# Segment attention on one NeuronCore: the value product moved ahead of the scores

## The chip, the cores and the metric

The kernel runs on one core of one Trainium2 chip. The metric is the device time of one execution in microseconds (us). Three executions of the kernel before took 755.57, 755.27 and 754.94 us; the median is 755.27 us.

## The reference

Two transformer layers act on 32 batches of 32 tokens of width 256 (1,024 tokens). The change concerns one block of the second layer, `_L1_attn_ref`: two self-attentions over the same tokens, one over all keys of a batch ("lt", long) and one over the keys of the token's own segment ("st", short), then a fusion.

```python
def _mha(x, w_in, b_in, w_out, b_out, n_heads, mask=None):
    qkv = x @ w_in.T + b_in
    q, k, v = jnp.split(qkv, 3, axis=-1)          # 16 heads of 16
    scores = jnp.einsum('bhqd,bhkd->bhqk', q, k) / jnp.sqrt(dh)
    if mask is not None:
        scores = jnp.where(mask[:, None, :, :], scores, -1e9)
    attn = jax.nn.softmax(scores, axis=-1)
    out = jnp.einsum('bhqk,bhkd->bhqd', attn, v)
    return out @ w_out.T + b_out
long_out = _mha(x, lt_w_in, ...)
seg = jnp.argmax(x @ protos.T, axis=-1)           # 8 segments
same = seg[:, :, None] == seg[:, None, :]
short_out = _mha(x, st_w_in, ..., mask=same)
short_out = jnp.where((tok_cnt == 1)[..., None], x, short_out)
combined = jnp.concatenate([long_out, short_out], axis=-1)
return combined @ fus_w.T + fus_b
```

Before it stand the first layer and a cross attention, behind it a layer of eight experts with two chosen for each token.

## The kernel before

The 1,024 tokens are 8 tiles of 128 tokens (4 batches each). Segment attention works in 16 units: unit n is tile n // 2, "lt" where n is even and "st" where it is odd. Each engine runs its own program of steps u, written out by hand in `pe_step`, `act_step`, `dve_step` and `pool_step`; engines meet only at semaphores, and each engine takes its own instructions in the order written. A step works on several units at once. Step u projects queries and keys of unit u+2, makes scores and the value product of unit u+1, and weighs the values of unit u. Even steps (s == 0) also make the segment logits of the next tile; odd steps (s == 1) transpose the one-hot segments of the next tile ("hot") and multiply them into the mask ("same").

One unit goes through the engines like this. TensorE: `project_qk` (helper line L837). ScalarE: kT (L2053) and qT (L2058) out of PSUM. GpSimd: the block-diagonal keys kbd (`spread_heads`, L853, two instructions). TensorE: the scores (`per_batch`, L877, 32 small matmuls) into `s_banks`. VectorE: `off_maximum` (L2219, L2220 for even units; L2226, L2230, L2231 for odd ones). ScalarE: the exponential (L2023). VectorE: `turn`, a transpose (L914). Beside this TensorE makes the value product (`project_tokens`, L846) into `v_part`, ScalarE copies it out (`act_v`, L2008) and GpSimd spreads it (`spread_batches`, L860). TensorE weighs the values (`values`, L904), ScalarE copies the result (`act_own`, L2013, L2016), VectorE normalises and transposes it (`features`, L2188, L2189, L937). `last_y` (L2149, L2154), `act_y` (L2029), `short` (L2242), `fused_near`, `fused_far` (L2161, L2167) and `add` (L2248) finish a tile. `norm_stats` (L2173 to L2176), `root` (L1973) and `norm_apply` (L2182) prepare a tile three ahead.

The value product shares PSUM bank 1 with three other results, the logits (L2107), the transposed one-hot (L2102) and the mask product (L2119). They take turns: each writer waits on the semaphore `vb_done` until the one before it has been read. The turns are counted by `v_use`, in this order:

```python
            if there(t + 1):
                v_use[("logits", "hot")[s], t + 1] = len(v_use) + 1
            if there(u + 1, U):
                v_use["v", u + 1] = len(v_use) + 1
            if s == 1 and there(t + 1):
                v_use["same", t + 1] = len(v_use) + 1
```

So in an even step the value product waits until VectorE has read the logits (`argmax`, L2200 and L2201; L2201 releases them), in an odd step until ScalarE has copied the one-hot (L2045), and the mask product waits until ScalarE has copied the value product (L2008). In `dve_step` the order is `features`, `turn`, `argmax`, `norm_stats` or `norm_apply`, then `off_maximum`.

Seven even steps have logits (u from 0 to 12). They are called logit steps below, the first to the seventh; their L2201 begin at 506.14, 518.23, 532.15, 545.45, 558.62, 571.80 and 586.51 us.

Of the kernel before, what the change touches and what calls it, by code (L numbers as in the profile page):

```python
# [25 lines left out]
NB, SQ, D, SK = 32, 32, 256, 257  # L26
# [40 lines left out]
def at_least(eng, sem, value):  # L67

    if isinstance(value, int) and value <= 0:
        return  # L70
    eng.wait_ge(sem, value)
# [770 lines left out]
def project_tokens(nc, dst, lhs_T, weight):  # L842

    n = weight.shape[1]
    for k in range(n):
        ins = nc.tensor.matmul(dst[:, 0:D], lhs_T[:, k, :], weight[:, k, :], start=(k == 0), stop=(k == n - 1))  # L846
    return ins
# [21 lines left out]
def per_batch(nc, dst, left, right, col, first):  # L869

    for m in range(KT):
        for b in range(BT):
            for f in range(2):
                lo, at = 64 * f, col + P * m
                ins = nc.tensor.matmul(dst[SQ * b:SQ * b + SQ, f, at:at + P], left(lo, m, b), right(lo, m, b),  # L877
                                       start=first and m == 0, stop=True, skip_group_check=True)
    return ins


def tokens(xT):

    return lambda lo, m, b: xT[lo:lo + 64, m, SQ * b:SQ * b + SQ]


def heads_apart(bd):

    return lambda lo, m, b: bd[lo:lo + 64, m, b, :, :].rearrange("p h k -> p (h k)")
# [1013 lines left out]
class SegmentAttention:  # L1903


    def __init__(self, nc, in_wn, in_shared, sem, psum, bank, c, x, w, loaded):
# [4 lines left out]
        def sb(name, shape):  # L1911
            return (in_wn if name in IN_WN or name[0:-1] in IN_WN else in_shared).take(shape)

        column, xT = in_shared.take([P, KT]), in_shared.take([P, NT, KT, P])
        self.turned, self.kept_end = xT, in_shared.at
        U = 2 * NT
        kinds = ("lt", "st")
# [5 lines left out]
        v, vbd = sb("v", [P, D]), [sb(f"vbd{i}", [P, 2 * NG, 2, 33]) for i in range(2)]  # L1923
# [13 lines left out]
        v_part, same_part = v_bank[:, 0:D], v_bank[:, D:D + SQ]  # L1937
# [8 lines left out]
        vb_full, vb_done = sem("vb_full"), sem("vb_done")  # L1946
# [8 lines left out]
        f_use, v_use = {}, {}  # L1955
# [136 lines left out]
        def pe_step(pe, u):  # L2092
# [21 lines left out]
            if there(u + 1, U):  # L2114
                scores(pe, u + 1)
# [14 lines left out]
                fused_far(pe, t - 1)  # L2130

        def scores(pe, n):
            pe.wait_ge(kbd_ready, n + 1)
            pe.wait_ge(q_ready, n + 1)
            at_least(pe, s_read, n)
            per_batch(nc, s_banks, tokens(qT[n % 2]), heads_apart(kbd[n % 2]), 0, True).then_inc(s_full, 1)
            at_least(pe, vb_done, v_use["v", n] - 1)
            project_tokens(nc, v_part, xT[:, n // 2], w[kinds[n % 2] + "_qkv"][:, :, 2 * D:3 * D]) \
                .then_inc(vb_full, 1)

        def values(pe, n):
            pe.wait_ge(pT_ready, n + 1)
# [802 lines left out]
```

## Time and profile before

| | before |
|---|---|
| median of 3 executions | 755.27 us |
| span of the profiled execution, first to last instruction | 751.1 us |
| segment attention's scores, first to last | 500.3 to 597.7 us |
| TensorE busy over the span | 662.8 us (88%) |
| VectorE busy over the span | 485.5 us (65%) |
| ScalarE busy over the span | 365.0 us (49%) |
| GpSimd busy over the span | 310.1 us (41%) |

The span is what the profiler saw of one execution. The profile gives no device time of its own for it; the median of the executions is 4.2 us longer than its span. In the views PE is TensorE's matmuls, PEld its weight loads, DVE VectorE, ACT ScalarE, POOL GpSimd. The value product is two matmuls in the program; the trace shows four, since fp32 matmuls appear in passes.

### The profile page before, as it was taken

Reading aid. Unit: us, or ns where it says so; the run is one execution under the profiler, and the core shown is the slowest. Engines: PE = TensorE matmul, PEld = TensorE weight load, DVE = VectorE, ACT = ScalarE, POOL = GpSimd, SP = SyncE. Lnnn points to the kernel's source line nnn. Section 1 sums busy time; section 2 is a strip of 40 time slices with the busy share of each in tenths; the row PEclk is TensorE's granted clock in tenths of the full one; section 3 lists DMA queues with packets and bytes.
Section 4 is the critical chain, followed back from the end, with each engine's and each line's share of the span. In section 5 each row is a group of like instructions: output and inputs, shape, how many; then the busy total and the mean of one; then the engine's idle time right before and its main releaser. Section 6 shows DMA issues by size and latency. Waiting matters only on the chain.

```text
span 751.1 us, 16917 instructions
## 1 busy us (share of the span) xinstructions
PE 662.8 (88%) x6115; PEld 500.4 (67%) x6115; DVE 485.5 (65%) x1367; ACT 365.0 (49%) x992; POOL 310.1 (41%) x458
## 2 busy tenths in 40 slices
PE   4899999999999989985994799988999776999990
PEld 3677878787777778753443586667877673777760
DVE  2686777677768669885488873558888875333330
ACT  1454545545555479874395653436566431222320
POOL 1235455646453179850000031136556513556541
PEclk9999999999999999996997699999999986999995
DMA  8723222322220000019200434538001022243434
GB/s 265 245 62 79 64 78 65 78 65 75 68 72 14 1 3 4 3 44 332 103 0 1 156 125 177 217 125 367 2 3 65 3 99 53 47 69 58 68 40 70
DMA packets 31697, 65.08 MB, mean 87 GB/s; under 512 B 5792, under 2 KB 21792, under 8 KB 29312
## 3 DMA queue, kind: packets, MB, share of 16 engines
q1 hardware_dynamic: 26016, 55.73, 22.8%
q0 software_dynamic: 4688, 7.18, 6.0%
q10 hardware_dynamic: 912, 1.10, 0.5%
q8 instruction: 50, 0.82, 0.5%
q14 instruction: 31, 0.25, 0.1%
HBM read 57.67 MB, written 7.37 MB: 87 GB/s over the span
## 4 chain that ended last, share of the span: by engine, by line
PE 64%; DVE 21%; ACT 5%; issue 4%; DMA 2%; SPq 2%; POOL 1%; DVEq 0%; ACTq 0%; POOLq 0%
PE psum L2627 7%; PE psum L474 6%; PE psum L482 6%; PE psum L496 5%; PE psum L2637 4%; PE psum L521 4%; PE psum L507 4%; PE psum L1482 3%; PE psum L1459 3%; PE psum L837 2%; DVE ff_peak L1500 2%; PE psum L846 2%; PE psum L829 2%; PE psum L877 2%; DMA wn<-in_w_down 2%
## 5 line engine op out<-in xcount | busy, mean ns | idle before, releaser
L415 ACT ACTIVATE prob<-s_sb,negm 128x257 f32<-128x257 f32 x128 | 66.2, 517 | 94.5 <-DVE negm L640 94.5
L782 POOL TENSOR_SCALAR bias<-dist,cst 128x257 f32<-128x257 f32 x128 | 59.8, 486 | 99.5 <-DVE dist L627 89.6
L636 DVE CUSTOM_DVE_ANT_0 s_sb<-psum,bias 128x257 f32<-128x257 f32 x128 | 49.4, 423 | 51.7 <-PE psum L496 48.4
L474 PE MATMUL psum<-ctxT,shared 128*128 128x257 f32 x256 | 62.6, 388 | 2.7 <-DMA msk<-in_mask 2.7
L482 PE MATMUL psum<-shared,ctxT 128*128 128x256 f32 x256 | 60.4, 379 | 0.0
L2627 PE MATMUL psum<-ex_w,shared 128*128 x184 | 58.3, 460 | 0.6 <-ACT shared L2520 0.6
L1721 POOL TENSOR_TENSOR wn<-wn,cst 128x1 f32<-128x1 f32 x8 | 4.7, 589 | 120.4 <-DVE wn L1848 120.4
L474 PEld LDWEIGHTS psum<-ctxT,shared 128*128 128x128 f32 x256 | 47.2, 195 | 9.0 <-issue 3.4
L482 PEld LDWEIGHTS psum<-shared,ctxT 128*128 128x128 f32 x256 | 48.4, 189 | 6.8
L496 PE MATMUL psum<-kT,qbd 64*128 64x257 f32 x256 | 48.4, 429 | 3.0 <-DVE mx L636 2.9
L2627 PEld LDWEIGHTS psum<-ex_w,shared 128*128 128x128 f32 x184 | 33.1, 190 | 15.4 <-issue 0.8
L2810 DVE TENSOR_TENSOR shared<-psum,shared 128x352 f32<-128x352 f32 x23 | 12.1, 525 | 48.2 <-ACT shared L2536 48.2
L1459 PE MATMUL psum<-shared,ff_used_up 128*128 128x512 f32 x96 | 41.6, 593 | 0.0
L853 POOL TENSOR_TENSOR shared<-shared,cst 128x512 f32<-128x512 f32 x32 | 35.0, 1115 | 7.8 <-ACT shared L2053 6.8
L521 PE MATMUL psum<-pT,v 128*64 128x128 f32 x512 | 35.0, 279 | 2.8 <-DVE o_keys L689 2.8
L2536 ACT ACTIVATE shared<-psum 128x352 f32<-128x352 f32 x23 | 10.7, 464 | 52.8 <-PE psum L2627 52.8
L521 PEld LDWEIGHTS psum<-pT,v 128*64 128x64 f32 x512 | 27.4, 136 | 13.2 <-issue 13.1
L507 PE MATMUL psum<-cst,prob 128*128 128x128 f32 x256 | 35.0, 280 | 0.0
L496 PEld LDWEIGHTS psum<-kT,qbd 64*128 64x128 f32 x256 | 22.3, 184 | 18.6 <-DVE mx L636 10.1
L2637 PE MATMUL psum<-ex_w,shared 128*128 x138 | 33.7, 380 | 0.8 <-DVE shared L2801 0.8
L507 PEld LDWEIGHTS psum<-cst,prob 128*128 128x128 f32 x256 | 27.4, 141 | 10.5 <-issue 10.5
L837 PE MATMUL psum<-shared,late 128*128 128x128 f32 x256 | 33.2, 285 | 0.0
(359 smaller groups left out, 1655.9 us busy)
## 6 DMA issues: line engine op xcount, KB each, us to landing
ctxT<-in_ctx_T SPq DMA_DIRECT2D x32, 257.0 KB
ex_w<-in_w SPq DMA_DIRECT2D x1, 5632.0 KB, 17.5
kpos<-in_kpos SPq DMA_DIRECT2D x32, 128.5 KB
msk<-in_mask SPq DMA_DIRECT2D x32, 128.5 KB
near_turned<-in_ctx_T_tiles SPq DMA_DIRECT2D x4, 1028.0 KB
ff_used_up<-in_ctx_T_tiles SPq DMA_DIRECT2D x4, 1028.0 KB
near_rows<-in_ctx_tiles SPq DMA_DIRECT2D x4, 1024.0 KB, 8.0
ff_used_up<-in_ctx_tiles SPq DMA_DIRECT2D x4, 1024.0 KB, 7.3
```

Source lines behind the costliest of these rows:

```text
L415: nc.scalar.activation(prob[n % 2][:, g, :], s_sb[n % 2][:, g, :], ACT.Exp, bias=negm[:, b, g:g + 1], accum_out=esum[t % 2][:, b, g:g + 1]) \
L474: ins = nc.tensor.matmul(kv[m][:, 0:SK], w["xa_k"][:, k, P * m:P * m + P], ctxT[n % BT][:, k, :], start=(k == 0), stop=(k == KT - 1))
L482: ins = nc.tensor.matmul(kv[0][:, D * i:D * i + D], ctxT[n % BT][:, k, P * i:P * i + P], w["xa_v"][:, k, :], start=(i == 0 and k == 0), st ...
L496: nc.tensor.matmul(sc[g % 2][:, 0:SK], qbd[t % 2][lo:lo + 64, g // 2, b, :, :].rearrange("p h q -> p (h q)"), kT[n % 2][lo:lo + 64, g // 2 ...
L507: ins = nc.tensor.transpose(pt[j][:, at:at + P], prob[n % 2][:, g, P * i:P * i + P], c.ident)
L521: ins = nc.tensor.matmul(oo[64 * half:64 * half + 64, at:at + P], v[n % BT][:, i, 64 * g:64 * g + 64], pT[n % 2][:, g, i, :], start=(n % 2 ...
L636: nc.vector.tensor_tensor_reduce(s_sb[n % 2][:, g, :], sc[g % 2][:, 0:SK], bias[n % 2][:, g, :], 1.0, float("-inf"), ALU.add, ALU.max, mx[ ...
L782: nc.gpsimd.tensor_scalar(bias[n % 2][:, g, :], dist[n % 2][:], c.slope[:, g:g + 1], 1.0, ALU.mult, ALU.mult).then_inc(bias_ready, 1)
L837: ins = nc.tensor.matmul(dst[:, P * m:P * m + P], weight[:, k, P * m:P * m + P], xT[:, k, :], start=(m == 0 and k == 0), stop=True, skip_g ...
L1459: ins = nc.tensor.matmul(bank[2 + n % 6][:], wt[:, k, P * m:P * m + P], xT[:, k, 512 * h:512 * h + 512], start=(k == 0), stop=(k == KT - 1))
L2627: ins = nc.tensor.matmul(y_bank[part][:, 0:FE], rT[j % 2][:, k, :], ex.w1[:, bass.ds(e, 1), k, FE * part:FE * part + FE].rearrange("p a f ...
L2637: ins = nc.tensor.matmul(o_bank[j % 2][:, 0:D], gT[j % 2][0:n, ch, :], ex.w2[0:n, bass.ds(e, 1), ch, :].rearrange("p a d -> p (a d)"), sta ...
```

## The change

In `scores` the value product and its wait are written ahead of the scores and their waits. Nothing else is altered; the counts of `v_use` stay.

```diff
         def scores(pe, n):
+            at_least(pe, vb_done, v_use["v", n] - 1)
+            project_tokens(nc, v_part, xT[:, n // 2], w[kinds[n % 2] + "_qkv"][:, :, 2 * D:3 * D]) \
+                .then_inc(vb_full, 1)
             pe.wait_ge(kbd_ready, n + 1)
             pe.wait_ge(q_ready, n + 1)
             at_least(pe, s_read, n)
             per_batch(nc, s_banks, tokens(qT[n % 2]), heads_apart(kbd[n % 2]), 0, True).then_inc(s_full, 1)
-            at_least(pe, vb_done, v_use["v", n] - 1)
-            project_tokens(nc, v_part, xT[:, n // 2], w[kinds[n % 2] + "_qkv"][:, :, 2 * D:3 * D]) \
-                .then_inc(vb_full, 1)
```

On TensorE a logit step reads as follows, with - for before and + for after; the rows are the logits, queries and keys, scores (L877), value product (L846), the values of the unit before, and the first product of `last_y`.

```order
 L2107 MATMUL psum<-late,shared 128x8 x2
 L837 MATMUL psum<-shared,late 128x128 x8
-L877 MATMUL psum<-shared 32x128 x16
-L846 MATMUL psum<-late,shared 128x256 x2
+L846 MATMUL psum<-late,shared 128x256 x2
+L877 MATMUL psum<-shared 32x128 x16
 L904 MATMUL psum<-shared,wn 64x2x33 x16
 L2149 MATMUL psum<-shared 128x128
```

The value product, with the wait that it carries, has gone ahead of the 32-column scores and stands directly behind the queries and keys. An odd step, with the transposed one-hot (L2102) ahead and the mask product (L2119) behind, reads:

```order
 L2102 MATMUL psum<-cst,shared 8x128
 L837 MATMUL psum<-shared,late 128x128 x8
-L877 MATMUL psum<-shared 32x128 x16
-L846 MATMUL psum<-late,shared 128x256 x2
+L846 MATMUL psum<-late,shared 128x256 x2
+L877 MATMUL psum<-shared 32x128 x16
 L2119 MATMUL psum<-shared 32x32 x4
 L904 MATMUL psum<-shared,wn 64x2x33 x16
```

Here the scores have come between the value product and the mask product. This exchange is made 16 times, once for each unit. The orders of VectorE, ScalarE, GpSimd and the DMA queues are the same as before.

## Rows read from the trace of the kernel before

**Rows 1.** The page: busy us (share of the span) of each engine
```profile
PE 662.8 (88%) x6115; PEld 500.4 (67%) x6115; DVE 485.5 (65%) x1367; ACT 365.0 (49%) x992; POOL 310.1 (41%) x458
```

**Rows 2.** Chain that ended last, 543 to 559 us: start, us, what
```profile
545.45 0.24 DVE shared L2201
...
547.03 0.70 DVE shared L2226
...
548.48 0.79 DVE shared L2231
...
550.66 0.46 DVE shared L2242
...
553.84 0.61 DVE shared L2219
```

**Rows 3.** Timeline of TensorE, fourth logit step and the odd step behind
```profile
542.75 2.03 PE L837 MATMUL psum<-shared,late 128*128 128x128 f32 x16
544.71 0.67 PE L877 MATMUL psum<-shared 64*32 64x128 f32 x32
545.73 1.13 PE L846 MATMUL psum<-late,shared 128*128 128x256 f32 x4 [0.35 <-DVE shared L2201]
546.79 0.70 PE L904 MATMUL psum<-shared,wn 64*64 64x66 f32 x32
...
551.44 1.13 PE L846 MATMUL psum<-late,shared 128*128 128x256 f32 x4
553.03 0.26 PE L2119 MATMUL psum<-shared 8*32 8x32 f32 x8 [0.46 <-ACT shared L2008]
```

**Rows 4.** Timeline, the first scores: TensorE's row and VectorE's
```profile
500.26 0.67 PE L877 MATMUL psum<-shared 64*32 64x128 f32 x32 [0.34 <-POOL shared L853]
...
501.03 0.69 DVE L2219 TENSOR_REDUCE shared<-psum 128x16 f32<-128x512 f32 x1 [1.72 <-PE psum L877]
```

**Rows 5.** Timeline of ScalarE, fourth logit step: exponential, copy of the one-hot
```profile
549.35 0.63 ACT L2023 ACTIVATE wn<-shared 128x512 f32<-128x512 f32 x1 [0.24 <-DVEq L2233]
...
550.77 0.25 ACT L2045 COPY shared<-psum 8x128 f32<-8x128 f32 x1
```

**Rows 6.** Timeline, second logit step: TensorE, VectorE and ScalarE
```profile
518.74 0.88 PE L877 MATMUL psum<-shared 64*32 64x128 f32 x32
...
519.81 0.69 DVE L2226 TENSOR_TENSOR shared<-psum,shared 128x512 f32<-128x512 f32 x1
...
522.95 0.63 ACT L2023 ACTIVATE wn<-shared 128x512 f32<-128x512 f32 x1
```

**Rows 7.** Timeline, sixth logit step: VectorE and GpSimd
```profile
573.08 0.68 DVE L2226 TENSOR_TENSOR shared<-psum,shared 128x512 f32<-128x512 f32 x1
574.10 1.04 POOL L860 TENSOR_TENSOR shared<-shared,cst 128x512 f32<-128x512 f32 x1
574.51 1.17 DVE L2231 TENSOR_TENSOR shared<-shared 128x512 f32<-128x512 f32 x1
```

**Rows 8.** Timeline of VectorE and TensorE, seventh logit step
```profile
586.51 0.23 DVE L2201 TENSOR_SCALAR shared<-psum,shared 128x8 f32<-128x8 f32 x1
588.02 0.68 DVE L2226 TENSOR_TENSOR shared<-psum,shared 128x512 f32<-128x512 f32 x1
...
586.79 1.13 PE L846 MATMUL psum<-late,shared 128*128 128x256 f32 x4 [1.34 <-DVE shared L2201]
```

**Rows 9.** Timeline of GpSimd, fourth logit step: the two spreads of the keys
```profile
547.67 2.48 POOL L853 TENSOR_TENSOR shared<-shared,cst 128x512 f32<-128x512 f32 x2
```

**Rows 10.** The same, in a stretch that ends within the pair
```profile
547.67 1.04 POOL L853 TENSOR_TENSOR shared<-shared,cst 128x512 f32<-128x512 f32 x1
```

**Rows 11.** Waits, 480 to 625 us: total us, times, longest
```profile
PEld psum L2119 <- ACT shared L2008: 6.9, 8, 0.9
```

**Rows 12.** Stretch of 5 us (third from last: mean granted clock); TensorE's longest wait
```profile
600.00:605.00 5.00, 3.74 (x46) 3.62 (x47) 4.49 (x11) 2.32 (x7) 2.25 (x6) 0.66 0.01 3
...
601.26 1.16 PE L904 MATMUL psum<-shared,wn 64*64 64x66 f32 x32 [2.20 <-DVE wn L914]
```

## The prediction

> **What bounds the kernel now.** First the page's busy times: TensorE is busy for 88% of the span and VectorE for 65% [rows 1]. By this alone an exchange on TensorE that keeps its work the same should cost nothing, and TensorE would be the engine to relieve. The chain of waits says otherwise for this stretch. In segment attention the work that ends last runs through VectorE: the release of the logits (L2201), the odd unit's scores off their maximum (L2226 and L2231), through ScalarE to `short` (L2242), and later the even unit's scores (L2219) [rows 2]. Its only break in a pair of steps lies between the end of L2231 at 549.27 and L2242 at 550.66, where ScalarE takes the exponential and then `act_y`. The timeline of TensorE shows the reverse side: in the same pair it waits twice, 0.35 us ahead of the value product, for L2201, and 0.46 us ahead of the mask product, for ScalarE's copy of the value product [rows 3]. So VectorE, with ScalarE's exponential between, sets the pace, and TensorE has about 0.8 us to spare in the 13.2 from one logit step to the next. What counts is when TensorE hands VectorE its scores.
>
> **The change, part by part.** Nothing is added or removed. The value product takes 1.06 us from its start to the start of what follows (545.73 to 546.79) [rows 3], and 16 scores are put behind it. The exchange itself is worth nothing: the same two blocks take their time in either order. I judge each unit by when its scores now arrive and when VectorE wants them.
>
> How late can scores be? VectorE waited for scores once: they began at 500.26 and VectorE's L2219 at 501.03 [rows 4]. From the start of scores to the start of VectorE's work on them is thus 0.77 us.
>
> *Logit steps (seven).* Here the value product waits for L2201. That was so before too, but the scores had already gone: 544.71 in the fourth logit step, when L2201 had not begun [rows 2, 3]. Now they queue behind the waiting product. L2201 begins at 545.45 and the product 0.28 us later; 1.06 us later come the scores, and 0.77 us later L2226. That is 0.28 + 1.06 + 0.77 = 2.11 us from the start of L2201 to the start of L2226, where it was 547.03 - 545.45 = 1.58 us [rows 2]. The work of VectorE between them (three small operations and the statistics of `norm_stats`) covers only the 1.58. So L2226 comes 0.53 us later. The exponential waited for VectorE's L2231 (0.24 us of idle time, on VectorE's queue [rows 5]), so all of it is passed on: to the exponential, `act_y`, L2242 and the next step. The values of the old unit come 0.6 us later on TensorE as well, but ScalarE's copies had 0.24 us in hand and the exponential gets 0.53 us more, so they still end in time.
>
> Then a second effect. GpSimd's two spreads of the keys took 2.48 us together, the first 1.04 us [rows 9, 10], so the second took 1.44. L2231 began at 548.48, ahead of the first one's end at 548.71, and took 0.79 us, where L2226, of the same size with one input from PSUM, takes 0.69 [rows 6]; in the sixth logit step it began at 574.51, in the middle of GpSimd's L860 that ended at 575.14, and took 1.17 us [rows 2, 7]. In both cases it ended some 0.5 to 0.6 us after GpSimd's instruction, and in the first GpSimd's next one paid the rest. I read this as: of these two kinds of instruction the one that starts later stands until the other ends, less about 0.13 us. Now L2231 would begin at 549.01, inside the second spread, which undisturbed runs to 548.71 + 1.04 = 549.75. It would start work near 549.6 and take 0.6 us more than 0.69, 0.5 us more than before. Under the Trainium skill ("SBUF — State Buffer", the section on the ports) a VectorE instruction with two SBUF inputs and a GpSimd instruction that reads SBUF exclude each other, and whichever starts first holds the ports to its end. By that rule the step pays about 0.5 us beyond the delay of the scores; if the rows' long L2231 were chance, 0. The trace agrees with the rule in these two rows.
>
> So the first, third, fourth and fifth logit steps, which are alike, cost 0.53 + 0.5 = 1.0 us each, 4.0 in all; the bounds are 0.53 (no meeting, 2.1 in all) and 1.1. The other three differ.
> - Second: TensorE is late itself. Its scores began at 518.74, so now the value product begins there, the scores at 519.8 and L2226 at 520.57 in place of 519.81, 0.76 us later [rows 6]. But the exponential at 522.95 did not wait for VectorE; L2231, 1.45 us after L2226, ended near 522.04. Its new end is near 522.7 without a meeting and 523.1 with one. 0 to 0.3 us; I take 0.2.
> - Sixth: L2226 came 573.08 - 571.80 = 1.28 us behind L2201 (there are no statistics between), so it is 0.83 us late [rows 7]. But L2231 then begins at 575.34, after GpSimd's end at 575.14, and loses its 0.48 us of standing. 0.83 - 0.48 = 0.35 us; bound 0.83.
> - Seventh: 588.02 - 586.51 = 1.51, so 0.60 us [rows 8].
>
> *Odd steps (eight) and the last even one.* The value product waits for the one-hot, which ScalarE has copied by 551.02 [rows 5]. From there: product at 551.07, scores at 552.13, L2219 possible at 552.90. It stood at 553.84 in the chain [rows 2]; the delay is hidden behind VectorE's own transposes and `norm_apply`, with 0.9 us in hand. Were that cover gone, each would cost up to 0.6 to 0.7 us. The first odd step (the scores at 500.26, for which VectorE waited) has no cover at L2219 and gets it about 0.65 us later [rows 4]; the small operations behind it stood behind GpSimd before and can take up most. I take 0.1, bound 0.65. In the last even step TensorE has long idle time (2.20 us, [rows 12]) and I take 0.
>
> *What is gained.* In the odd steps the value product is ready one block earlier, and the wait ahead of the mask product, 6.9 us in eight on the weight loads [rows 11], should mostly vanish. TensorE is not on the path there, so I count 0. If the earlier values let each odd exponential start 0.2 us earlier and that were on the path, it would be worth 1.6 us at most.
>
> **Sum.** 4.0 + 0.2 + 0.35 + 0.6 + 0.1 = 5.25 us; less 0.15 for a few tenths that standing instructions in the odd steps take up: 5.1 us. The span of the profiled execution would go from 751.1 to 756.2 us. The median of the runs lies 4.2 us above the span, and I add the same 5.1 us to it: 755.27 + 5.1 = 760.4 us.
>
> **Rivals.**
> *A, the forecast:* the scores come late in the logit steps, with the meeting of L2231 and GpSimd or without. With it 760.4. Without it the sum is 2.1 + 0.05 + 0.35 + 0.6 + 0.1 = 3.2, so 758.5. For it: L2226 has no idle time ahead of it and lies on the chain.
> *B, hidden:* the delay goes into waiting time that was there anyway, as in the second logit step, where TensorE set the exponential. If that were so in all seven, 7 x 0.05 to 0.2 = 0.4 to 1.4 us: 755.7 to 756.7. Against it: the exponential's 0.24 us on VectorE's queue [rows 5].
> *C, the clock:* TensorE's waits become one longer one. In 600 to 605 us the mean granted clock was 0.66, part of it at 1.2 GHz and not 2.4, and there L904 took 1.16 us for its usual 0.70, behind 2.20 us of idle time [rows 3, 12]. In the seventh logit step TensorE idled 1.34 us after the scores [rows 8]; now the scores' 0.67 us join that, and with what it runs ahead the gap is 2.0 to 2.3 us. If the clock falls there, product and scores (1.7 us) take about 1.66 times as long, 1.1 us more, and the values behind them some 0.5 us: 762.0. If it falls in the steps with gaps near 1.1 us too, 765 or more.
> *D, faster:* the shorter path from value product to mask product counts more than the scores. If TensorE's order is what sets the pace, 8 waits of 0.46 us vanish [rows 3, 11], 3.7 us, against at most 1.4 us of B: 753 us. It decides for faster where L2226 finds its scores within 1.58 us of L2201, that is, if the value product began over half a microsecond earlier than L2201 lets it. Against it: L846 waited for exactly that.
>
> **How the numbers follow.** A holds 0.72 (0.45 with the meeting, 0.27 without or with part of it), C 0.14, B 0.09, D 0.05. The likeliest case gives 760.4. The range goes from 757.6, a little under A without the meeting, to 762.4, above the milder C; some 0.2 lie outside. About 0.2% (1.5 us) is what a measurement of this kernel can tell from no change. Slower by more than that: A, C and a little of B, 0.88; within it 0.08; faster 0.04.
>
> **What would show it.** In the profile after: L846 ahead of L877 with all of TensorE's wait for L2201, about 1.1 us; L2226 at 2.1 us behind L2201 with idle time ahead of it put down to L877; L2231 at 1.2 to 1.3 us in four logit steps; L2219 without idle time; L2119 without its wait for L2008; and the stretch from the first scores to the last longer by 5 us. The prediction is wrong if L2226 has no idle time ahead of it, if L2231 stays at 0.8 us (then 758.5), or if the granted clock falls in a stretch where it was full.

## The result and the profile after

The changed kernel takes 760.12 us (median of six) against 754.87 us for the kernel before on the same chip. That is 5.25 us slower, where 5.1 were forecast, 760.4 us. One of the six runs, 817.51 us at a lower clock, is left out of the comparison: the median of the other five is 759.93 us, 5.1 slower, the ratio 1.0078, 95% interval 1.0058 to 1.0098. Timed again later, the same kernel took 758.26 us against 754.33, ratio 1.0058 (1.0039 to 1.0076), 3.9 us slower. The profiled execution's span is 757.4 us, and its own time 759.15 us, 1.75 us more. By the same distance the profiled execution of the kernel before, with its span of 751.1 us, took about 752.9 us (an estimate), 2.4 under its median: so the two profiles differ by 6.3 us, more than the medians do.

The page of the changed kernel, busy times of each engine: TensorE's share is as it was [rows 1].

```profile
span 757.4 us, 16917 instructions
PE 665.1 (88%) x6115; PEld 502.6 (66%) x6115; DVE 486.7 (64%) x1367; ACT 365.1 (48%) x992; POOL 309.9 (41%) x458
```

What changed is who waits. The chain that ended last, around the fourth logit step (start, us, what), answers to [rows 2]:

```profile
548.84 0.24 DVE shared L2201
549.12 1.13 PE psum L846 x4
550.25 0.68 PE psum L877 x32
550.96 0.70 DVE shared L2226
551.68 0.70 DVE shared L2230
552.41 1.25 DVE shared L2231
...
555.05 0.45 DVE shared L2242
```

TensorE's product and scores now stand in the chain between L2201 and L2226, where VectorE's own small operations stood before. L2226 begins 550.96 - 548.84 = 2.12 us behind L2201; the forecast had 2.11, the kernel before 1.58. It is so in six of the seven logit steps. L2231 takes 1.25 us in place of 0.79.

The timelines of TensorE, VectorE and GpSimd in the same step answer to [rows 3, 9]:

```profile
549.12 1.13 PE L846 MATMUL psum<-late,shared 128*128 128x256 f32 x4 [0.73 <-DVE shared L2201]
550.18 0.67 PE L877 MATMUL psum<-shared 64*32 64x128 f32 x32
...
557.12 0.26 PE L2119 MATMUL psum<-shared 8*32 8x32 f32 x8
...
550.96 0.69 DVE L2226 TENSOR_TENSOR shared<-psum,shared 128x512 f32<-128x512 f32 x1 [0.49 <-PE psum L877]
552.41 1.24 DVE L2231 TENSOR_TENSOR shared<-shared 128x512 f32<-128x512 f32 x1
...
551.06 2.04 POOL L853 TENSOR_TENSOR shared<-shared,cst 128x512 f32<-128x512 f32 x2
553.06 1.49 POOL L860 TENSOR_TENSOR shared<-shared,cst 128x512 f32<-128x512 f32 x1
```

VectorE now idles 0.49 us ahead of L2226 for the scores. The mask product L2119 has lost its wait, as forecast, and nothing comes of it. The two spreads of the keys take 2.04 us, undisturbed, where the kernel before had 2.48; L2231 began inside the second one (it ended at 553.10) and then L860 stood until L2231 had ended. The waits, in total us, times and longest:

```profile
PEld psum L846 <- DVE shared L2201: 7.4, 7, 2.1
...
DVE shared L2226 <- PE psum L877: 4.8, 7, 1.6
...
PEld psum L846 <- ACT shared L2045: 4.6, 6, 1.4
```

In the seventh logit step something else joins. TensorE's timeline there, and the windows of 5 us (third number from the end is the mean granted clock):

```profile
588.50 2.03 PE L837 MATMUL psum<-shared,late 128*128 128x128 f32 x16
592.47 1.77 PE L846 MATMUL psum<-late,shared 128*128 128x256 f32 x4 [1.94 <-DVE shared L2201]
594.17 1.11 PE L877 MATMUL psum<-shared 64*32 64x128 f32 x32
595.21 1.15 PE L904 MATMUL psum<-shared,wn 64*64 64x66 f32 x32
...
590.00:595.00 5.00, 3.06 (x41) 1.93 (x40) 3.52 (x12) 1.51 (x5) 2.86 (x4) 0.78 0.00 0
595.00:600.00 5.00, 5.00 (x77) 4.51 (x62) 2.75 (x6) 3.29 (x11) 0.77 (x1) 0.88 0.01 3
```

Product, scores and values take 1.77, 1.11 and 1.15 us where they take 1.13, 0.67 and 0.70 elsewhere: this is the lower level, 1.2 GHz (from 592.5 to 596.4 us the mean granted clock is 0.56), behind 1.94 us of idle time. In the same step the kernel before ran at full clock.

### The profile page after: what moved, and what is told of

Same layout as the page of the kernel before. It is cut to its first block, busy times and chain, and to the rows that moved or that the text cites. A ratio compares the mean times of both kernels' runs of the same rounds, so it can differ in the third digit from the quotient of the medians.

```text
span 757.4 us, 16917 instructions
## 1 busy us (share of the span) xinstructions
PE 665.1 (88%) x6115; PEld 502.6 (66%) x6115; DVE 486.7 (64%) x1367; ACT 365.1 (48%) x992; POOL 309.9 (41%) x458
## 4 chain that ended last, share of the span: by engine, by line
PE 68%; DVE 21%; issue 4%; ACT 3%; DMA 2%; POOL 1%; SPq 0%; DVEq 0%; ACTq 0%; POOLq 0%
PE psum L474 7%; PE psum L2627 7%; PE psum L482 7%; PE psum L496 6%; PE psum L2637 4%; PE psum L521 4%; PE psum L507 4%; PE psum L846 3%; PE psum L1482 3%; PE psum L1459 3%; PE psum L877 2%; DVE ff_peak L1500 2%; PE psum L829 2%; PE psum L837 2%; DVE wn L914 1%
## 5 line engine op out<-in xcount | busy, mean ns | idle before, releaser
L853 POOL TENSOR_TENSOR shared<-shared,cst 128x512 f32<-128x512 f32 x32 | 32.7, 1042 | 11.0 <-ACT shared L2053 11.0
L846 PE MATMUL psum<-late,shared 128*128 128x256 f32 x96 | 27.6, 411 | 10.2 <-DVE shared L2201 6.1
```

## The experiments

All were run against the kernel before on the same chip. "Pair" is the time from the start of L2201 in the fourth logit step to that in the fifth, from the profile; before it was 558.62 - 545.45 = 13.17 us, in the changed kernel 14.13.

| run | median us | before | ratio (95% interval) | pair us |
|---|---|---|---|---|
| e1 product first in logit steps | 759.78 | 754.21 | 1.0080 (1.0049 to 1.0112) | 14.13 |
| e2 product first in odd steps | 754.08 | 754.21 | 1.0000 (0.9981 to 1.0019) | 13.18 |
| e3 the wait alone first | 755.45 | 754.21 | 1.0029 (1.0009 to 1.0050) | 13.46 |
| e4 logits read ahead of `turn` | 754.16 | 754.19 | 1.0008 (0.9995 to 1.0020) | 13.19 |
| e5 logits in columns of their own | 755.07 | 754.21 | 1.0010 (0.9994 to 1.0025) | 13.13 |
| e6 `root` behind the spreads | 758.16 | 754.19 | 1.0065 (1.0048 to 1.0082) | 13.78 |
| e7 matmuls in the gap | 758.56 | 754.19 | 1.0065 (1.0046 to 1.0085) | 14.14 |
| e8 before, `norm_apply` moved | 754.02 | 754.19 | 0.9999 (0.9983 to 1.0015) | 12.81 |
| e9 changed, `norm_apply` moved | 757.87 | 754.33 | 1.0048 (1.0033 to 1.0063) | 13.76 |
| e10 e8 and e2 together | 753.53 | 754.33 | 0.9984 (0.9966 to 1.0003) | 12.80 |
| e11 changed, e8 and e4 together | 752.86 | 754.33 | 0.9976 (0.9955 to 0.9996) | 12.81 |
| e12 the changed kernel again | 758.26 | 754.33 | 1.0058 (1.0039 to 1.0076) | 14.13 |

### Which steps cost: e1 and e2

```diff
 def scores(pe, n):
-    (value product)
+    if n % 2 == 1: (value product)     # e1; in e2 n % 2 == 0
     (waits and scores)
+    if n % 2 != 1: (value product)     # e2: n % 2 != 0
```

> The value product goes ahead of the scores for the short units alone, that is in the seven logit steps and the last even one. Theory A (the scores queue behind a product that waits for the logits' release, and the later L2231 then meets GpSimd): all of the cost is here, 5 to 6 us over before, about 760; L2226 at 2.11 us behind L2201. If the odd steps had a share in it, less than 759.

> The value product goes ahead of the scores for the long units alone, that is in the odd steps. Theory A: the delay is hidden behind VectorE's own work, -0.3 to +0.3 us against before. Rival D (TensorE's shorter way to the mask product is worth its wait): up to 3.7 us faster than before.

e1 has the whole cost, 5.6 us, and the pair of the changed kernel to 0.01 us. e2 has none, in time and in the pair. The theory stands, and rival D falls: in e2 the mask product's wait is gone too (in seven of the eight odd steps; the first keeps 0.37 us) and the kernel is not faster.

### Wait or length: e3 and e5

```diff
 # e3, from the kernel before
 def scores(pe, n):
+    at_least(pe, vb_done, v_use["v", n] - 1)
     (waits and scores)
-    at_least(pe, vb_done, v_use["v", n] - 1)
     project_tokens(...)
 # e5, from the changed kernel (t + 1 > 0)
+    apart = y_bank[:, D + P:D + P + NE]
-    matmul(logits, ...).then_inc(vb_full, 1)
+    matmul(apart, ...).then_inc(lg_full, 1)
+    pe.wait_ge(lg_done, t + 1)          # ahead of last_y, same bank
```

> Only the wait on vb_done moves ahead of the scores; the product stays behind them. Theory A: scores can begin 0.28 us behind L2201 and L2226 0.77 us after that, 1.05 us in all, inside the 1.58 us that VectorE is busy anyway: no change, within 0.5 us of before. Rival (the wait itself is what costs, the product's length does not matter): most of the 5 us stays.

> The order of the changed kernel, but the logits of tiles 1 to 7 have 8 columns of their own in PSUM bank 4 and semaphores of their own, so that the value product does not wait for their release in the logit steps. Theory A: the product begins directly behind the queries and keys, the scores 1.06 us later, before VectorE wants them; L2226 at 1.58 us behind L2201 again, time within 0.7 us of before. Rival (the product's 1.06 us ahead of the scores costs by itself): most of the 5 us stays.

e5 went as expected, within its interval: with the length of the product ahead of the scores but without the wait, the pair is 13.13 us and L2231 takes 0.78 us again. From e5's timelines, TensorE and VectorE around its fourth logit step (its L2207, L2208 and L2233 are L2200, L2201 and L2226 of the other kernels):

```profile
546.94 1.03 PE L846 MATMUL psum<-late,shared 128*128 128x256 f32 x4
547.90 0.67 PE L877 MATMUL psum<-shared 64*32 64x128 f32 x32
...
548.08 0.23 DVE L2208 TENSOR_SCALAR shared<-psum,shared 128x8 f32<-128x8 f32 x1
...
549.66 0.69 DVE L2233 TENSOR_TENSOR shared<-psum,shared 128x512 f32<-128x512 f32 x1
```

The product begins 1.14 us ahead of L2208 and L2233 follows L2208 by 1.58 us. So in the steps that are alike neither the order nor the product's 1.06 us costs; they cost only behind the wait. Two other steps are a little longer than before: the sixth by 0.15 us (14.86) and the seventh by 0.55 (15.17). In the seventh VectorE never waits for scores; its small operation L2214 takes 0.77 us for the usual 0.23 beside a spread of GpSimd. The second step ran in part at 1.2 GHz, as before.

e3 missed its expectation, which was no change: the pair is 0.29 us longer and the kernel 0.1 to 0.5% slower, though L2226 is at 1.58 us and L2231 at 0.78. The chain of e3 in its fourth logit step tells why:

```profile
546.72 0.24 DVE shared L2201
...
547.00 0.67 PE psum L877 x32
547.67 1.06 PE psum L846 x4
548.73 0.67 PE psum L904 x32
...
549.49 0.36 ACT wn L2016
...
550.64 0.36 issue
551.00 0.47 ACT wn L2023
...
552.31 0.45 DVE shared L2242
```

A second branch leads from L2201 to the exponential L2023: scores, product, the old unit's values (L904), and ScalarE's copies of them (L2016), which are ahead of the exponential in ScalarE's queue. The values begin 548.66 - 546.72 = 1.94 us behind L2201, in the kernel before 546.79 - 545.45 = 1.34 us [rows 2, 3]. These 0.60 us less the 0.24 us that the exponential had waited before [rows 5] are 0.36, near the 0.29 of the pair. In the changed kernel the values come at the same 1.94 us (550.78 to 548.84), but there L2231 ends later still and hides this branch.

### Is it where the logits are read: e4

```diff
 def dve_step(dve, u):
+    if s == 0 and there(t + 1): argmax(dve, t + 1)
     if there(u, U): turn(dve, u)
-    if s == 0 and there(t + 1): argmax(dve, t + 1)
```

> The order of the changed kernel, and in VectorE's step the reading of the logits goes ahead of the transpose (turn) in place of behind it. Theory A: L2201 releases the value product 0.6 us earlier while VectorE's own work ahead of the scores grows from 1.58 to 2.2 us behind it, and 2.11 us then fit in: L2226 without idle time, L2231 at 0.8 us, time within 1 us of before (754 to 755). Rival (the product's 1.06 us of TensorE ahead of the scores costs wherever the logits are read): stays near 760.

As expected: 754.16 us, pair 13.19, and in the steps that are alike L2226 comes 2.17 us behind L2201, with VectorE busy all the time between. Only in the sixth step, which has no statistics, does L2226 still wait for scores, 0.61 us; the step is 14.71 us as before, since L2231 takes 0.91 us there in place of 1.17. With this one exchange on VectorE the changed order is free. The price lay in when the release comes, not in TensorE's work.

### The meeting of L2231 and GpSimd: e6

```diff
 def pool_step(pool, u):
-    if s == 0 and ...: root(pool, t + 3)
     (two spread_heads)
+    if s == 0 and ...: root(pool, t + 3)      # for u >= 0
```

> The changed kernel, with GpSimd's rstd (root) behind the two spreads of the keys in the even steps, so that the spreads end before L2231 begins. Theory A with the meeting of L2231 and GpSimd worth 0.5 us in five steps: L2231 at 0.69 us, L2226 still 2.11 us behind L2201, about 2.5 us faster than the changed kernel: 757.5. Rival (L2231's 1.24 us is not GpSimd's doing): L2231 stays, 760.

Half met. From e6's timeline (its L2233 is L2231 of the others):

```profile
549.46 1.04 POOL L860 TENSOR_TENSOR shared<-shared,cst 128x512 f32<-128x512 f32 x1
...
550.21 0.83 DVE L2233 TENSOR_TENSOR shared<-shared 128x512 f32<-128x512 f32 x1
```

With the spreads out of the way L2231 falls from 1.24 to 0.83 us and the pair from 14.13 to 13.78, while L2226 stays at 2.12 us. The rest is a new meeting: it begins inside L860, 0.29 us ahead of that one's end. I had overlooked that L860 moves up too. The first two logit steps of this profile are 0.4 and 0.7 us longer (13.35 and 14.75 against 12.91 and 14.06), but they say nothing of `root`: TensorE ran at 1.2 GHz in both, the queries and keys took 3.44 and 3.26 us for 2.03, and the product came late without waiting for L2201. The medians (758.16, and 758.26 to 760.12 for the changed kernel) can't tell the two apart; the pair can.

### The clock: e7 and e12

```diff
 def scores(pe, n):
+    if n == 13:
+        at_least(pe, s_read, n)
+        keep_busy(nc, s_banks[:, 0, 0:D], xT[:, n // 2, 0, :], w["st_qkv"][:, 0, 2 * D:3 * D], 3)
     (value product, waits and scores)
```

> The changed kernel, with three extra matmuls of 128x256 (1.6 us) into the empty score banks in the seventh logit step, where TensorE waited 1.94 us for L2201 and then ran product, scores and values at 1.2 GHz. The results are overwritten by the scores. If the idle time is what the clock fell for: L846 at 1.06 to 1.13 us in that step, the step 1.5 us shorter, 758.6 to 759.5. If the clock falls there whatever TensorE does: no change, or slower by what the extra matmuls push back.

> The changed kernel once more, for a second profile and more timed runs. If the 1.2 GHz stretch in its seventh logit step belongs to the kernel, it is there again and that step is again 16.7 us to the last L2226; if it is a matter of the single execution, 15.24 us as in the two variants that had the same order there. Time 758.5 to 760.5.

The second profile of the changed kernel shows the slow stretch in the same place:

```profile
590.32 1.81 PE L846 MATMUL psum<-late,shared 128*128 128x256 f32 x4 [1.94 <-DVE shared L2201]
592.06 1.10 PE L877 MATMUL psum<-shared 64*32 64x128 f32 x32
```

From L2201 there to the last L2226 it is 16.73 us, in the first profile 16.71; the timed median, 758.26 us, lies 0.2 us under the range expected. With e7's extra matmuls it is 15.24 us, with L846 at 1.13 us; that would be 1.47 us for the clock. But e1, e6 and e9 have the same 1.94 us of idle time ahead of L846 and no extra matmuls, and L846 at 1.13 us, as this row of e1 shows (its L2206 is L2201 of the others):

```profile
589.70 1.13 PE L846 MATMUL psum<-late,shared 128*128 128x256 f32 x4 [1.94 <-DVE shared L2206]
```

So the stretch costs 1.5 us where it comes, it came in both profiles of this kernel, and its idle time alone does not bring it. For the same reason e7 does not show that its extra matmuls kept the clock up. e7's timed median, 758.56 us, lies between the two of the changed kernel and decides nothing. What brings it stays open.

### VectorE's pace, and a better order: e8 to e11

```diff
 def dve_step(dve, u):
-    if s == 1 and there(t + 3) and t + 3 >= 2: norm_apply(dve, t + 3)
+    if s == 1 and t + 3 == 2: norm_apply(dve, t + 3)
     if there(u + 1, U): off_maximum(dve, u + 1)
+    if s == 0 and there(t + 3) and t + 3 >= 3: norm_apply(dve, t + 3)
```

This is e8 on the kernel before and e9 on the changed one; e10 adds e2's order to e8, e11 adds e4's to e9.

> The kernel before (scores first), with norm_apply (L2182) of tiles 3 to 7 moved from the odd step, ahead of the even unit's scores, to the even step behind the odd unit's scores, where VectorE idles 1.40 us for ScalarE. Theory A says that VectorE's own work between the scores sets the pace there: each move takes 0.4 to 1.1 us off the path, 4.3 us in the five steps, about 750. Rival (TensorE has only 0.8 us in 13.2 to spare and becomes the bound): 1 to 3 us faster and longer waits of VectorE for L877.

> The changed kernel, with norm_apply moved to the even step behind the odd unit's scores, as in the kernel before with the same move. Theory A: VectorE's chain loses up to 1.1 us in five steps but L2226 still comes 2.11 us behind L2201, so the cost of the change stays and time lies 2 to 5 us under the changed kernel, 755 to 758. Rival (once VectorE has less to do, TensorE sets the pace and the exchange costs less or nothing): below 755.

> The kernel before, with norm_apply moved to the even step and the value product ahead of the scores in the odd steps alone. With norm_apply moved the time from one logit step to the next was 12.81 us, TensorE without a wait but the 0.46 us ahead of the mask product, which the exchange in the odd steps takes away. If TensorE sets that pace: 12.4 us a pair, 2 us less than with the move alone, 751 to 752. If VectorE sets it: 12.8, no change against the move alone.

> The changed kernel, with norm_apply moved and the logits read ahead of the transpose: all three orders together. If L2201 comes early enough for the product in a step of 12.8 us or less, the time is that of the kernel before with norm_apply moved or up to 2 us less, 751 to 753. If the scores come late again (2.11 us behind L2201 against VectorE's 2.2 us), 754.

e8 missed its expectation: 754.02 us against 754.19, where about 750, or by the rival 1 to 3 us faster than before, was expected. The other three came out by one of the two cases named: e9 at 757.87 us keeps the cost, e10 has no change against the move alone, e11 lies at 752.86. The move of `norm_apply` into VectorE's wait for ScalarE shortens the pair from 13.17 to 12.81 us, less than the 1.06 us that L2182 held of the chain there (552.78 to 553.84): the wait ahead of `short` shrinks from 1.40 to 0.36 us and L2182 takes 0.83 us, still standing for GpSimd. The stretch from the first logit step's L2201 to the last L2226 is 1.8 us shorter in e8's profile (93.22 against 94.99). But 1.11 us of this stand in the second logit step (12.81 against 13.92), where the kernel before ran at 1.2 GHz for a while and e8 did not, so the move itself is worth about 0.7 us there. The timed runs show no difference of the whole, and by their interval the gain is at most 0.2%. The cost of the change is the same beside it: 13.76 - 12.81 = 0.95 us a pair, as 14.13 - 13.17 = 0.96. e10's pair equals e8's, so TensorE's wait for the mask product does not set even that pace. e11 is the only version faster than before by its interval, by 0.04 to 0.45%, 1.5 us in the medians. Its pair is no shorter than e8's, and one such interval out of twelve that misses 1 by so little is weak evidence; that e11 is faster is not shown for certain, and where the difference would lie is not shown at all.

## Why the prediction was right, and where it was not

Times of the steps from L2201 to the next L2201 (for the seventh, to the last L2226), from the profiles:

| logit step | before | after | difference | forecast |
|---|---|---|---|---|
| 1 | 12.09 | 12.91 | +0.82 | 1.0 |
| 2 | 13.92 | 14.06 | +0.14 | 0.2 |
| 3 | 13.30 | 14.13 | +0.83 | 1.0 |
| 4 | 13.17 | 14.13 | +0.96 | 1.0 |
| 5 | 13.18 | 14.14 | +0.96 | 1.0 |
| 6 | 14.71 | 15.08 | +0.37 | 0.35 |
| 7 | 14.62 | 16.71 | +2.09 | 0.60 |

- *The delay of L2226* (0.28 + 1.06 + 0.77 = 2.11 us). Right to 0.01 us; e4 and e5 take it away in two ways.
- *The meeting of L2231 with GpSimd* (0.5 us in five steps, or nothing). Right for the steps forecast: 1.24 us in the first five, 0.69 in the sixth, which had 1.17 before. In each meeting of the profiles before and after L2231 ends 0.54 to 0.55 us behind the instruction of GpSimd that it met (553.65 behind 553.10 in the fourth step); in the sixth it begins 0.23 us behind the end of L860 and takes its plain 0.69. e6 moves the meeting away in part and gets back 0.35 us of the pair. The rule of the Trainium skill ("SBUF — State Buffer", the section "Who interferes with whom") is that of a VectorE instruction with two SBUF inputs and a GpSimd instruction that reads SBUF, the one that issues second is blocked until the first has finished. The trace agrees: L2231 was the second in each of these meetings and was the one that stood.
- *The second step.* The size was right and the reason wrong. I took TensorE's lateness there (scores at 518.74 [rows 6]) as given. It came from a stretch at a lower clock, queries and keys in 3.39 us for 2.03, as TensorE's row and the window (third number from the end: mean granted clock) of the kernel before show:

```profile
515.42 3.39 PE L837 MATMUL psum<-shared,late 128*128 128x128 f32 x16
515.00:520.00 5.00, 5.00 (x54) 4.55 (x55) 4.54 (x16) 2.36 (x7) 0.82 (x2) 0.66 0.85 365
```

This is gone in both profiles of the changed kernel. The step pays its full 1.0 us, and about 0.86 come back from the clock; that is the difference of the two, and e4's second step, at full clock, is 0.80 us shorter than that of the kernel before (13.12 against 13.92). Whether the change is what took the stretch away is not shown: it also came in the profiles of e2, e5, e6, e10 and e11 and not in those of e1, e3, e4, e7, e8 and e9. The value product there waits for L2201 like the others, as these rows of the changed kernel show:

```profile
518.04 2.03 PE L837 MATMUL psum<-shared,late 128*128 128x128 f32 x16
520.93 1.13 PE L846 MATMUL psum<-late,shared 128*128 128x256 f32 x4 [0.85 <-DVE shared L2201]
```

- *The seventh step.* The 0.60 us of the mechanism are there: in e1, without the slow stretch, the step is 15.24 us, 0.62 over before. The other 1.47 us are the milder case of rival C, priced at 1.6. It was also a sign of being wrong by the prediction's own last sentence, since the granted clock was full in this step before (1.00 in the windows from 585 to 600 us): A and this part of C came together, which the sum of A did not hold.
- *The odd steps.* Hidden, as forecast (e2). The 0.1 us for the first is 0: from the L2201 of tile 0 to that of tile 1 it is 10.12 us in the changed kernel and in e8, which has the order of before there (in the kernel before's own profile it is 10.31).
- *The wait ahead of the value product.* 1.1 us were named as a sign; it is 0.73 in the fourth step and 0.37 to 1.94 over the seven. Nothing in the sum hung on it.
- *"They still end in time."* True of the changed kernel, but only since L2231 ends so late. e3 shows that the later values cost 0.3 us a pair by themselves once the scores don't hide them; the prediction had no such branch, and my expectation for e3 missed for that.
- *The total.* From the first logit step to the last L2226 the profile is 6.17 us longer: 5.56 us of the mechanism in the seven steps (with 1.0 for the second and 0.62 for the seventh), less 0.86 and plus 1.47 us by the clock. The forecast for the seven was 5.15, with the second step at 0.2; steps 1 and 3 were estimated 0.2 too high each. The timed runs give 5.25 and 3.9 us. What lies outside the stretch differs between executions: it began 1.6 us later in the profile after, and the part behind it was 1.5 us shorter. So the mechanism was right and sized to about half a microsecond, but that the total fell within 0.2 us of the forecast is luck: the profiles hold two pieces of the clock of opposite sign that the sum did not have, and a second timing of the same kernel gave 1.3 us less.

## What to carry to other kernels

A wait costs with all that is queued behind it on its engine. Ahead of an exchange, ask of each moved instruction what releases it, and add from that release to the consumer; neither block's length nor the wait alone would have cost as much here. Follow every branch that leaves the release (here scores, and values by way of ScalarE's queue): removing the later one can uncover the next. And a shift of half a microsecond can double itself where it slides an instruction of one engine into one of another that it has to wait out; one can see it in the rows by an instruction that takes longer than its shape does elsewhere (here 1.24 us for 0.69) and ends a fixed time behind the other engine's (here 0.55 us). Last, take a forecast apart step by step even when its total comes out: here two pieces of the clock of opposite sign were hidden in it.

## What the runs showed that was not expected

TensorE's granted clock did not follow the length of one idle time. Behind the same 1.94 us it fell in two profiles and stayed full in three others (e1, e6, e9). And the changed kernel, with more idle time between 510 and 521 us (1.23, 1.19 and 0.85 us in its timeline) than the kernel before had (0.46, 0.46 and 1.00 us), ran at full clock there where the kernel before fell to a mean of 0.66 between 515 and 520 us. What brings such a stretch is open, and it can move a single step (by 1.47 us) more than the change does.
